# First attention in five units a batch with packed diagonal squares, up-biases with the experts' weights, rotations by one projection and a shuffle

## The chip, the cores and the metric

One core of a Trainium2 chip runs the whole program. The metric is the device time of one execution in microseconds, the median of several runs of the same kernel.

## The reference, cut to what matters

Two layers over x of 32 batches x 256 tokens x 128 channels, float32. The change is in layer 0:

```python
xn = layernorm(x)
# attention without softmax, 16 heads of 8 channels
q1, k1, q2, k2 = (rotary((xn @ W.T).reshape(B, T, 16, 8)) for W in (Wq1, Wk1, Wq2, Wk2))
v = (xn @ Wv.T).reshape(B, T, 16, 8)
# rotary on halves of a head: y1 = x1*cos + x2*sin ; y2 = -x1*sin + x2*cos
s1, s2 = q1 @ k1, q2 @ k2                      # per head, 256 x 256
pattern = where(causal, s1 / 8 * (s2 / 8), 0)
s = (pattern @ v) @ Wout.T
# gate: 8 experts, best 2 of each token, sigmoid scores
up = xn @ up_w[e] + up_b[e]                    # 128 -> 512
eo = gelu(up) @ down_w[e] + down_b[e]
g = silu(shared_expert(xn) + 0.1 * sum(w_e * eo_e))
x = x + s * g
```

Layer 1 (a strided softmax attention and a second mixture of experts) is as it was.

## The kernel before, in words

The kernel is written by hand for each engine: `tensor_program` (TensorE, PE), `vector_program` (VectorE, DVE), `scalar_program` (ScalarE, ACT), `gpsimd_program` (GpSimd, POOL) and `sync_program` (SyncE, SP, which issues most DMAs, all on one hardware queue). Each is one list of instructions in order, tied to the others by semaphores, so an engine that waits holds up all that stands behind in its own list.

**Stages.** 0 to 51 us: x is loaded, normalised, turned onto channels (XT), and values and gate logits are made (L1655 to L1663). 51 to 519 us: the first attention. To 767 us: 71 slabs of 256 rows through the experts (`expert_pe`, L1871 up and L1880 down; weights by L443, rows by L469). Then the shared expert and end of layer 0, and from 915 us on layer 1.

**The first attention** runs over 32 batches (NB) in NU = 6 x 32 units. The 256 keys x 256 queries of a batch are taken as three pairs of 128-blocks: keys low/queries low, low/high, high/high. The fourth pair lies above the diagonal and is left out. Two units make a pair, and each does 8 heads: a head group r (32 channels, four heads) stands on 32 partitions, and the queries are held in QM in four masked copies, one a head, so that one product of 32 rows x 128 keys with 4 x 128 = 512 columns gives the scores of four heads. A unit has two of these products of each kind (s1 and s2), t = 0 and 1, on row groups 2(n%2) + t, each into a PSUM bank of its own. `score_units` (L1684) issues in each step, for t = 0, 1: s1 of the next unit, then s2 of this one. The next and this unit use different row groups, so a step's four products stand on the four row groups of the array (shape 32*128 in the profile).

ScalarE copies s1 of a unit out of PSUM (L823, two instructions of 512 columns), GpSimd sets what lies above the diagonal to zero in the four units of the diagonal pairs (`causal`, L663, with a lower bound of zero), VectorE multiplies by s2 into PP (L1538), and `weigh_first` (L1708, shape 128*32) multiplies with the values VM: for each pair 16 products of 128 columns, four column groups side by side. VM is a masked copy of the values (L814), and the result is copied out once a batch (L989).

**Rotations.** Each of the four (q1, k1, q2, k2 of a batch) is two projections of 256 columns (`projection`, L1648 by W and L1649 by W with the halves of each head swapped on the host), one VectorE product of 512 columns with cos and sin (L1280), and a sum, for keys on VectorE (L1285), for queries on GpSimd (`query_sum`, L657). ScalarE makes the four masked copies of the queries (L801). They are made one to two batches ahead.

**Beside it** the gate's routing advances on VectorE by a table (`route_step`), with counts and ranks on TensorE in `ROUTED_BY` batches, and from unit 56 on GpSimd sends 2 x 64 x 128 rows to the experts' lists by 128 indirect DMAs (L630). The last steps of the routing build a table UB of the up-biases of each slab (L1214 to L1225, eight rounds), which `expert_act` reads; `s.ub` is raised after it, and `expert_weights` waits for that.

**The queue of SP** at the start: x, W0, cos/sin, then 17 DMAs of zeros into xd and 8 into yd (L578), then up_b (L580), two small matrices of the ranks (L581, L582), then a wait for all zeros, `turn_counts` (L506), weights, and rows of the experts.

## Time and profile before

| | |
|---|---|
| median of 3 runs | 1614.48 us (1612.23 to 1617.23) |
| the profiled execution's own time | 1612.6 us |
| its span, first to last instruction | 1611.4 us |
| PE / PE weight loads / DVE / ACT / POOL busy | 94% / 69% / 61% / 61% / 52% |
| first attention | 51 to 519 us |
| PE busy in it | 453.55 of 468 us |

Busy time is not work at peak: products are pipelined and a record's end is modelled, so starts of successive groups say more than lengths. A float32 product leaves two records on PE and two weight loads: the 192 x 4 products of `score_units` are 1536 records in the rows below.

### The profile page before, as it was taken

Reading aid. Unit: us, or ns where it says so; the run is one execution under the profiler, and the core shown is the slowest. Engines: PE = TensorE matmul, PEld = TensorE weight load, DVE = VectorE, ACT = ScalarE, POOL = GpSimd, SP = SyncE. Lnnn points to the kernel's source line nnn. Section 1 sums busy time; section 2 is a strip of 40 time slices with the busy share of each in tenths; the row PEclk is TensorE's granted clock in tenths of the full one; section 3 lists DMA queues with packets and bytes.
Section 4 is the critical chain, followed back from the end, with each engine's and each line's share of the span. In section 5 each row is a group of like instructions: output and inputs, shape, how many; then the busy total and the mean of one; then the engine's idle time right before and its main releaser. Section 6 shows DMA issues by size and latency. Waiting matters only on the chain.

```text
span 1611.4 us, 46794 instructions
## 1 busy us (share of the span) xinstructions
PE 1517.2 (94%) x18059; PEld 1107.6 (69%) x18059; DVE 981.5 (61%) x2063; ACT 986.3 (61%) x2039; POOL 831.8 (52%) x908
## 2 busy tenths in 40 slices
PE   7999999999999999999999889999998999999895
PEld 5545454555544999999778656666666999997663
DVE  6788898877776222222599968756664222225887
ACT  5766666777766555445455557677776545455773
POOL 7334488888875555555112210277764555553433
PEclk9999999999999999999999989999999999999998
DMA  9910002110002899999344320011113545532434
GB/s 314 418 66 2 7 30 78 51 32 30 30 26 36 217 247 253 253 247 240 92 118 118 85 56 3 15 48 47 47 43 55 95 91 99 93 76 80 133 108 126
DMA packets 296954, 169.45 MB, mean 105 GB/s; under 512 B 198080, under 2 KB 273216, under 8 KB 293792
## 3 DMA queue, kind: packets, MB, share of 16 engines
...
## 4 chain that ended last, share of the span: by engine, by line
PE 63%; POOL 12%; issue 10%; DVE 7%; ACT 4%; DMA 2%; SPq 1%; POOLq 0%; DVEq 0%; ACTq 0%
PE ps L1880 14%; PE ps L1871 14%; POOL xd L630 6%; POOL s_S L663 4%; PE ps L1684 4%; PE ps L1775 4%; PE ps L1812 4%; PE ps L1912 4%; ACT s_PX L889 3%; PE ps L1900 3%; DVE s_RS L1350 3%; PE ps L1708 2%; PE ps L1822 2%; PE ps L1841 2%; PE ps L1648 2%
## 5 line engine op out<-in xcount | busy, mean ns | idle before, releaser
L630 POOL DMA_INDIRECT xd<-s_XN,s_slots x256 | 251.7, 983 | 83.9 <-issue 62.3
L823 ACT ACTIVATE s_S<-ps 128x512 f32<-128x512 f32 x384 | 208.4, 595 | 141.3 <-PE ps L1684 141.3
L1538 DVE TENSOR_TENSOR s_PP<-ps,s_S 128x1024 f32<-128x1024 f32 x192 | 234.4, 1221 | 74.1 <-PE ps L1684 52.7
L1684 PE MATMUL ps<-s_QM,s_KK 32*128 32x512 f32 x1536 | 233.8, 639 | 2.7 <-ACT s_S L823 2.7
L889 ACT ACTIVATE s_PX<-ps,s_scl 128x1024 f32<-128x1024 f32 x128 | 135.7, 1111 | 110.5 <-PE ps L1822 110.5
L904 ACT ACTIVATE s_HH<-ps,s_LG 128x256 f32<-128x256 f32 x284 | 125.2, 474 | 122.0 <-PE ps L1871 122.0
L663 POOL TENSOR_SCALAR_AFFINE_SELECT s_S<-s_S 128x1024 f32<-128x1024 f32 x128 | 140.8, 1100 | 114.0 <-ACT s_S L823 113.4
L647 POOL DMA_INDIRECT yd<-s_Y,s_to x142 | 136.2, 959 | 122.2 <-DVE s_Y L1480 97.8
L1350 DVE TENSOR_REDUCE s_RS<-ps 128x8 f32<-128x1024 f32 x128 | 150.3, 1216 | 63.3 <-PE ps L1779 63.3
L904 ACT ACTIVATE s_XN<-ps,s_b1s 128x256 f32<-128x256 f32 x256 | 113.4, 474 | 115.1 <-PE ps L1871 111.1
L647 POOL DMA_INDIRECT yd<-s_XN,s_to x128 | 122.7, 959 | 117.5 <-DVE s_XN L1480 95.6
L1480 DVE TENSOR_TENSOR s_Y<-ps,s_W 128x256 f32<-128x256 f32 x71 | 30.1, 424 | 188.8 <-PE ps L1880 188.8
L1880 PEld LDWEIGHTS ps<-s_W,s_HH 128*128 128x128 f32 x1136 | 137.8, 192 | 3.6
L1880 PE MATMUL ps<-s_W,s_HH 128*128 128x128 f32 x1136 | 138.1, 275 | 0.0
L1871 PE MATMUL ps<-s_XG,s_W 128*128 128x256 f32 x568 | 134.8, 380 | 1.7 <-DMA s_W<-in_ew 1.0
L1708 PEld LDWEIGHTS ps<-s_PP,s_VM 128*32 128x32 f32 x3072 | 76.1, 109 | 84.8 <-DVE s_PP L1538 52.0
L1480 DVE TENSOR_TENSOR s_XN<-ps,s_b2s 128x256 f32<-128x256 f32 x64 | 27.2, 425 | 172.0 <-PE ps L1880 172.0
L1871 PE MATMUL ps<-s_XN,s_W 128*128 128x256 f32 x512 | 123.0, 384 | 4.1 <-DVE s_XN L1467 3.1
L1880 PEld LDWEIGHTS ps<-s_W,s_XN 128*128 128x128 f32 x1024 | 124.3, 192 | 3.3
L1880 PE MATMUL ps<-s_W,s_XN 128*128 128x128 f32 x1024 | 124.6, 275 | 0.0
L801 ACT ACTIVATE s_QM<-s_RQ,s_small 128x256 f32<-128x256 f32 x252 | 113.9, 507 | 0.4 <-issue 0.4
L1684 PEld LDWEIGHTS ps<-s_QM,s_KK 32*128 32x128 f32 x1536 | 74.1, 183 | 56.7 <-issue 56.1
...
## 6 DMA issues: line engine op xcount, KB each, us to landing
...
s_X<-xd SPq DMA_DIRECT2D x540, 32.0 KB
...
xd<-s_XN,s_slots POOLq DMA_INDIRECT x256
```

The costliest lines, as they stand in the source:

```text
L630: e.indirect_dma_start(out=xd, out_offset=bass.IndirectOffsetOnAxis(ap=m.slots[:, k, i:i + 1], axis=0), in_=m.XNp[:, i, 0:C + 1], in_offse ...
L647: e.indirect_dma_start(out=x.yd, out_offset=bass.IndirectOffsetOnAxis(ap=m.to[n][:, 2 * i + t:2 * i + t + 1], axis=0), in_=x.Y[i % 4][:, t ...
L663: e.affine_select(out=sel, in_=sel, pattern=[[0, 8], [1, P]], compare_op=ALU.is_ge, fill=0.0, base=0, channel_multiplier=-1).then_inc(s.ma ...
L801: i = e.mul(m.QM[b % 2][:, kind, j, :], m.RQ[q % 2][:], m.mk[j])
L823: e.mul(m.S1[u % 3][:, t * 512:(t + 1) * 512], m.PA[:, t * 512:(t + 1) * 512], 1.0 / 64.0).then_inc(s.ev1, 1)
L889: e.activation(m.PX[hp][:, 2 * half:2 * half + 2, :].rearrange("p r n -> p (r n)"), m.ps[:, (2 + 2 * half) * 512:(4 + 2 * half) * 512], AC ...
L904: e.activation(x.HH[i % 2][:, j, :], m.PS[j][:, 0:SL], func, bias=bias(i, j)).then_inc(s.eact, 1)
L1350: e.tensor_reduce(m.MM[b % 2][:, hf, 8 * rp:8 * rp + 8], m.ps[:, 1024 * rp:1024 * rp + 1024].rearrange("p (x n) -> p x n", x=8), AX.X, ALU ...
L1538: e.tensor_tensor(m.PP[u % 4][:], m.PB[u % 2], m.S1[u % 3][:], ALU.mult).then_inc(s.prod, 1)
L1684: return e.matmul(out, m.KK[k][32 * r:32 * r + 32, kind, kc * P:(kc + 1) * P], m.QM[k][32 * r:32 * r + 32, kind, :, qc * P:(qc + 1) * P], ...
L1871: e.matmul(PS[j][:, 0:SL], W[:, 0, j * P:(j + 1) * P], x.XG[i % 2][:], start=True, stop=True).then_inc(s.eup, 1)
L1880: ins = e.matmul(PS[4 + i % 2][:, c * P:(c + 1) * P], x.HH[i % 2][:, j, c * P:(c + 1) * P], W[:, 1, j * C:(j + 1) * C], start=(j == 0), st ...
```

## The change

1. **Units.** Five units a batch (UB = 5). The 64 x 64 squares on the diagonal of both diagonal pairs are packed into unit 0: all four head groups, keys 0 to 63 of each block, queries 0 to 63, with two head groups side by side in the halves of 128 partitions (`scores_packed`, products of 32 rows x 64 keys x 256 columns). Units 1 and 2 hold queries 64 to 127 of each block against all 128 keys of it (`scores_high`, two products of 256 columns in place of one of 512), units 3 and 4 the low/high pair as before (`scores_across`). The order inside `score_units` stays: t = 0: s1 of the next, s2 of this; t = 1 the same.
2. **Weighing.** `weigh_packed` (64 rows x 32 columns, 32 products of 64 columns, halved over two steps), `weigh_high` (32 products of 64 columns), `weigh_across` (16 of 128). Packed ones with c odd take the values from partitions 64 to 127, so the values of partitions 0 to 63 are moved there by four small DMAs a batch in SP's queue (`moved_values`), each waited for by `weigh_packed` through `s.v2`.
3. **Mask.** Three whole selects a batch with base 64, and a fourth on 64 partitions for the packed unit, which waits for the first.
4. **Rotations.** One projection of 256 columns; the DVE product reads it twice by a stride of zero; STREAM_SHUFFLE on VectorE exchanges the halves of each head on partitions (256 columns), then a subtraction.
5. **Biases.** up_b stands behind the experts' weights (EW 1152 to 1156 words), so the table UB and the DMA of up_b go.
6. **Schedules** of routing, counts and scatters follow the five units. In SP's queue `moved_values(0)` stands ahead of the wait for the zeros and `moved_values(1)` behind it; `turn_counts` comes at batch 4, the first five experts' weights at batch 10.

```diff
--- before.py
+++ after.py
-NU = NB * 6
+UB = 5
+NU = NB * UB
...
-ROUTED_BY = [6, 7, 8, 9]
+ROUTED_BY = [5, 6, 7, 8]
...
+def moved_values(e, m, s, b):
+
+    g = b // 2
+    e.wait_ge((s.va, s.vd)[g % 2], g // 2 + 1)
+    e.wait_ge(s.zvm, 3)
+    if b >= 1:
+        e.wait_ge(s.pv, 3 * (b - 1) + 1)
+    for h in range(4):
+        src = m.RS[0:64, b * 256:b * 256 + 256].rearrange("p (k r h d) -> p r h k d", k=4, r=2, h=4)[:, 1, h, :, :]
+        e.dma_start(m.VM[b % 2][64:128, 2, h:16:4, 8 * h:8 * h + 8], src).then_inc(s.v2, 16)
...
     e.wait_ge(s.const, 96)
-    e.dma_start(m.upb[:], a["up_b"].rearrange("e (p j) -> p e j", j=4)).then_inc(s.upb, 16)
     e.dma_start(m.r0.low[:], a["c_low"].bitcast(BF16)).then_inc(s.const, 16)
     e.dma_start(m.r0.ones[:], a["c_ones"].bitcast(BF16)).then_inc(s.const, 16)
-    e.wait_ge(s.zero, 272)
-    e.wait_ge(s.zero_y, 128)
-    turn_counts(e, m, s, m.r0, 0)
-    for i in range(m.x0.NWB):
-        expert_weights(e, m, s, i)
+    for b in range(NB):
+        moved_values(e, m, s, b)
+        if b == 0:
+            e.wait_ge(s.zero, 272)
+            e.wait_ge(s.zero_y, 128)
+        if b == ROUTED_BY[0] - 1:
+            turn_counts(e, m, s, m.r0, 0)
+        if b == 10:
+            for i in range(m.x0.NWB):
+                expert_weights(e, m, s, i)
...
     if q >= 2:
         e.wait_ge(s.qm, q - 1)
-    e.tensor_tensor(m.RQ[q % 2][:], rt[:, 0:256], rt[:, 256:512], ALU.add).then_inc(s.rq, 1)
+    e.tensor_tensor(m.RQ[q % 2][:], rt[:, 0:256], m.QX[:], ALU.subtract).then_inc(s.rq, 1)
 
 
 def causal(e, m, s, u):
-    sel = m.S1[u % 3][:].rearrange("p (b q) -> p b q", q=P)
+    sel = m.S1[u % 3][:].rearrange("p (b q) -> p b q", q=64)
     e.wait_ge(s.ev1, 2 * u + 2)
-    e.affine_select(out=sel, in_=sel, pattern=[[0, 8], [1, P]], compare_op=ALU.is_ge, fill=0.0, base=0,
+    e.affine_select(out=sel, in_=sel, pattern=[[0, 16], [1, 64]], compare_op=ALU.is_ge, fill=0.0, base=64,
                     channel_multiplier=-1).then_inc(s.mask, 1)
+    if u % UB == 0:
+        low = sel[0:64, :, :]
+        e.wait_ge(s.mask, 4 * (u // UB) + 1)
+        e.affine_select(out=low, in_=low, pattern=[[0, 16], [1, 64]], compare_op=ALU.is_ge, fill=0.0, base=0,
+                        channel_multiplier=-1).then_inc(s.mask, 1)
 
 
 def windows(e, m, s, b):
@@ -725,12 +741,12 @@
     places(e, m, s, m.x0, 0, 1)
     scatters = scatter_steps()
...
-    e.tensor_tensor(rt[:], m.PS[7], m.cs[:], ALU.mult).then_inc(s.rt, 1)
-    if x % 2 == 1:
+    e.tensor_tensor(rt[:].rearrange("p (k n) -> p k n", k=2), bcast(m.PS[7][:, 0:256], 1, 2),
+                    m.cs[:].rearrange("p (k n) -> p k n", k=2), ALU.mult).then_inc(s.rt, 1)
+    e.wait_ge(s.rt, i + 1)
+    if x % 2 == 0:
+        e.stream_shuffle(m.QX[:], rt[:, 256:512], [p ^ 4 for p in range(32)]).then_inc(s.swapped, 1)
+    else:
         if b >= 2:
-            e.wait_ge((s.sc1, s.sc2)[x // 2], (12, 6)[x // 2] * (b - 1))
-        e.wait_ge(s.rt, i + 1)
-        e.tensor_tensor(m.KK[b % 2][:, x // 2, :], rt[:, 0:256], rt[:, 256:512], ALU.add).then_inc(s.ka, 1)
+            e.wait_ge((s.sc1, s.sc2)[x // 2], (2 * UB, UB)[x // 2] * (b - 1))
+        e.stream_shuffle(m.KX[:], rt[:, 256:512], [p ^ 4 for p in range(32)]).then_inc(s.swapped, 1)
+        e.wait_ge(s.swapped, i + 1)
+        e.tensor_tensor(m.KK[b % 2][:, x // 2, :], rt[:, 0:256], m.KX[:], ALU.subtract).then_inc(s.ka, 1)
...
-    e.matmul(m.PS[7][:, 0:256], m.W0[:, 2 * x, :], xt, start=True, stop=True)
-    e.matmul(m.PS[7][:, 256:512], m.W0[:, 2 * x + 1, :], xt, start=True, stop=True).then_inc(s.proj, 1)
+    e.matmul(m.PS[7][:, 0:256], m.W0[:, x, :], xt, start=True, stop=True).then_inc(s.proj, 1)
...
+def scores_packed(e, m, k, kind, out, t):
+
+    for x in range(2):
+        for half in range(2):
+            r, at = 2 * t + half, P * x
+            i = e.matmul(out[64 * half:64 * half + 64, 256 * x:256 * x + 256], m.KK[k][32 * r:32 * r + 32, kind, at:at + 64],
+                         m.QM[k][32 * r:32 * r + 32, kind, :, at:at + 64], start=True, stop=True, skip_group_check=True)
+    return i
+
+
+def scores_high(e, m, k, kind, out, r):
+
+    for x in range(2):
+        i = e.matmul(out[:, 256 * x:256 * x + 256], m.KK[k][32 * r:32 * r + 32, kind, x * P:(x + 1) * P],
+                     m.QM[k][32 * r:32 * r + 32, kind, :, x * P + 64:(x + 1) * P], start=True, stop=True, skip_group_check=True)
+    return i
+
+
+def scores_across(e, m, k, kind, out, r):
+
+    return e.matmul(out, m.KK[k][32 * r:32 * r + 32, kind, 0:P], m.QM[k][32 * r:32 * r + 32, kind, :, P:2 * P],
+                    start=True, stop=True)
+
...
-        k, pair, r = (n // 6) % 2, (n % 6) // 2, 2 * (n % 2) + t
-        kc, qc = (0, 0, 1)[pair], (0, 1, 1)[pair]
+        k, v = (n // UB) % 2, n % UB
         out = (m.PB[n % 2] if kind else m.PA)[:, t * 512:(t + 1) * 512]
-        return e.matmul(out, m.KK[k][32 * r:32 * r + 32, kind, kc * P:(kc + 1) * P],
-                        m.QM[k][32 * r:32 * r + 32, kind, :, qc * P:(qc + 1) * P], start=True, stop=True)
+        if v == 0:
+            return scores_packed(e, m, k, kind, out, t)
+        if v < 3:
+            return scores_high(e, m, k, kind, out, 2 * (v - 1) + t)
+        return scores_across(e, m, k, kind, out, 2 * (v - 3) + t)
...
+def weigh_packed(e, m, s, b, heads):
+
+    PP = m.PP[(UB * b) % 4]
+    e.wait_ge(s.prod, UB * b + 1)
     e.wait_ge(s.vm, b + 1)
-    if pair == 0 and b >= 1:
+    e.wait_ge(s.v2, 64 * (b + 1))
+    if b >= 1:
         e.wait_ge(s.yt, b)
     for h in heads:
-        for c in range(4):
-            i = e.matmul(m.PS[6][32 * c:32 * c + 32, qc * P:(qc + 1) * P], m.VM[b % 2][:, kc, 4 * c + h, :],
-                         m.PP[(2 * q + c // 2) % 4][:, (c % 2) * 512 + h * P:(c % 2) * 512 + (h + 1) * P],
-                         start=(pair == 0 and h == 0), stop=(h == 3 and pair != 1), skip_group_check=True)
+        for x in range(2):
+            for c in range(4):
+                at = 512 * (c // 2) + 256 * x + 64 * h
+                lanes = slice(64 * (c % 2), 64 * (c % 2) + 64)
+                values = m.VM[b % 2][lanes, 2, 8 * x + 4 * (c // 2) + h, :] if c % 2 else m.VM[b % 2][lanes, x, 4 * c + h, :]
+                i = e.matmul(m.PS[6][32 * c:32 * c + 32, P * x:P * x + 64], values, PP[lanes, at:at + 64],
+                             start=(h == 0 and x == 0), stop=(h == 3 and x == 0), skip_group_check=True)
     if heads[-1] == 3:
         i.then_inc(s.pv, 1)
+
+
+def weigh_high(e, m, s, b):
+
+    e.wait_ge(s.prod, UB * b + 3)
+    for h in range(4):
+        for x in range(2):
+            for c in range(4):
+                at = (c % 2) * 512 + 256 * x + 64 * h
+                i = e.matmul(m.PS[6][32 * c:32 * c + 32, P * x + 64:P * x + 128], m.VM[b % 2][:, x, 4 * c + h, :],
+                             m.PP[(UB * b + 1 + c // 2) % 4][:, at:at + 64], start=False, stop=(h == 3 and x == 0),
+                             skip_group_check=True)
+    i.then_inc(s.pv, 1)
+
+
...
-        q, heads = pair_of(u)
-        if v == 5 and b + 2 < NB:
-            projection(e, m, s, b + 2, 1)
-        if q is not None:
-            weigh_first(e, m, s, q, heads)
         if v == 0 and b + 1 < NB:
             projection(e, m, s, b + 1, 2)
-        if v == 2 and b + 1 < NB:
-            projection(e, m, s, b + 1, 3)
-        if v == 3 and b + 2 in ROUTED_BY:
-            e.wait_ge(s.rt, 4 * (b + 1) + 4)
-            stage = ROUTED_BY.index(b + 2)
+        if v == 1 and b >= 1:
+            weigh_across(e, m, s, b - 1)
+        if v == 1 and b + 1 in ROUTED_BY:
+            e.wait_ge(s.rt, 4 * (b + 1) + 3)
+            stage = ROUTED_BY.index(b + 1)
             if stage == 0:
                 route_counts(e, m, s, m.r0, 0)
             elif stage == 1:
                 route_total(e, m, s, m.r0)
             else:
                 route_ranks(e, m, s, m.r0, 0, stage - 2)
+        if v == 2 and b + 1 < NB:
+            projection(e, m, s, b + 1, 3)
+        if v in (2, 3) and b < NB:
+            weigh_packed(e, m, s, b, (2 * v - 4, 2 * v - 3))
+        if v == 3 and b + 2 < NB:
+            projection(e, m, s, b + 2, 0)
+        if v == 4:
+            weigh_high(e, m, s, b)
         if v == 4 and b + 2 < NB:
-            projection(e, m, s, b + 2, 0)
+            projection(e, m, s, b + 2, 1)
```

## Rows read from the trace of the kernel before

**Rows 1.** Windows: the first attention and a part of the experts, busy us of each engine.

```profile
51.00:519.00 468.00, 453.55 (x5103) 233.29 (x5105) 384.14 (x453) 323.12 (x701) 312.39 (x318) 1.00 0.18 60
560.00:640.00 80.00, 80.00 (x547) 75.25 (x547) 18.15 (x49) 40.27 (x92) 43.13 (x46) 1.00 0.97 250
```

**Rows 2.** Timeline of PE, one batch: start us, us, instructions merged by line.

```profile
299.60 1.34 PE L1684 MATMUL ps<-s_QM,s_KK 32*128 32x512 f32 x8
300.87 0.70 PE L1648 MATMUL ps<-s_XT,s_W 128*128 128x256 f32 x2
...
301.93 1.14 PE L1684 MATMUL ps<-s_QM,s_KK 32*128 32x512 f32 x8
...
305.71 0.64 PE L1708 MATMUL ps<-s_PP,s_VM 128*32 128x128 f32 x16
306.28 0.70 PE L1648 MATMUL ps<-s_XT,s_W 128*128 128x256 f32 x2
...
307.34 1.14 PE L1684 MATMUL ps<-s_QM,s_KK 32*128 32x512 f32 x8
...
312.82 1.08 PE L1708 MATMUL ps<-s_PP,s_VM 128*32 128x128 f32 x32
313.84 1.34 PE L1684 MATMUL ps<-s_QM,s_KK 32*128 32x512 f32 x8
```

**Rows 3.** Costliest groups of 51 to 517 us: busy us, mean ns, idle before.

```profile
L1538 DVE TENSOR_TENSOR s_PP<-ps,s_S 128x1024 f32<-128x1024 f32 x191 | 233.2, 1221 | 73.1 <-PE ps L1684 52.7 <-PE ps L1708 13.4 <-POOL s_S L663 5.0
L663 POOL TENSOR_SCALAR_AFFINE_SELECT s_S<-s_S 128x1024 f32<-128x1024 f32 x128 | 140.8, 1100 | 114.0 <-ACT s_S L823 113.4
L630 POOL DMA_INDIRECT xd<-s_XN,s_slots x128 | 127.7, 998 | 30.6 <-issue 28.8 <-DVE s_slots L1159 1.4 <-POOL s_XN L636 0.3
L1648 PE MATMUL ps<-s_XT,s_W 128*128 128x256 f32 x244 | 84.9, 429 | 10.0 <-DVE s_RT L1280 9.4 <-DVE s_r0TS L1142 0.3
L657 POOL TENSOR_TENSOR s_RQ<-s_RT 128x256 f32<-128x256 f32 x61 | 45.1, 739 | 9.0 <-DVE s_RT L1280 7.8
```

**Rows 4.** Timeline of PE in the experts, where no shape changes.

```profile
564.23 1.89 PE L1871 MATMUL ps<-s_XG,s_W 128*128 128x256 f32 x8
565.96 0.27 PE L1880 MATMUL ps<-s_W,s_HH 128*128 128x128 f32 x1
```

**Rows 5.** Timeline of PE, the batch of rows 2, cut so that one score group falls apart into its records.

```profile
302.46 0.61 PE L1684 MATMUL ps<-s_QM,s_KK 32*128 32x512 f32 x4
303.00 0.70 PE L1648 MATMUL ps<-s_XT,s_W 128*128 128x256 f32 x2
```

**Rows 6.** Timeline of PE in layer 1: weighing products of 64 columns.

```profile
1108.55 1.10 PE L1841 MATMUL ps<-s_PX,s_VN 128*32 128x64 f32 x64
1109.58 0.39 PE L1812 MATMUL ps<-s_Q,s_KS 32*128 32x128 f32 x4
```

**Rows 7.** Line L1467: the nearest VectorE instruction to a shuffle; min/median/max ns.

```profile
L1467 DVE STREAM_TRANSPOSE s_XG<-s_X x71: 403/435/447, 518.2 to 763.1; 128x256 f32<-128x256 f32 x71
```

**Rows 8.** Timeline of SP's queue at the start: start us, us to issue.

```profile
64.62 2.21 SPq L580 DMA_DIRECT2D s_upb<-in_up_b  x1
66.88 18.21 SPq L581 DMA_DIRECT2D s_r0low<-in_c_low  x1
85.14 1.02 SPq L582 DMA_DIRECT2D s_r0ones<-in_c_ones  x1
```

**Rows 9.** DMA issues: KB each, median us from issue to landing.

```profile
s_r0low<-in_c_low SPq DMA_DIRECT2D x1, 32.0 KB, 20.7
s_r0ones<-in_c_ones SPq DMA_DIRECT2D x1, 32.0 KB, 5.1
```

**Rows 10.** Timeline of SP's queue: issues of rows' DMAs in the experts.

```profile
601.60 2.01 SPq L469 DMA_DIRECT2D s_X<-xd  x4
```

**Rows 11.** Timeline of PE: the first weighing of batch 0.

```profile
61.22 1.08 PE L1708 MATMUL ps<-s_PP,s_VM 128*32 128x128 f32 x32
```

**Rows 12.** Windows around a sparse stretch of PE: its granted clock is the last but two.

```profile
930.00:935.00 5.00, 3.24 (x23) 2.78 (x29) 2.82 (x12) 2.37 (x6) 0.00 (x0) 0.50 0.00 0
```

More of the change, by code:

```diff
@@ L53, in route_step @@
 def route_step(u):
-    if u < 25:
-        return 2 if u % 6 in (1, 3) else 0
-    if u < 61:
-        return {25: 1, 27: 1, 31: 1, 33: 1, 37: 1, 39: 1, 43: 1, 45: 1, 49: 2, 51: 1, 55: 1}.get(u, 0)
-    return 1 if u % 6 in (1, 3) else 0
+    if u < 20:
+        return {0: 1, 1: 2, 3: 1}.get(u % UB, 0)
+    return {20: 1, 21: 1, 23: 1, 26: 2, 31: 1, 33: 1, 36: 2, 38: 1, 40: 1, 41: 1, 43: 1, 45: 1}.get(u, 0)
 def scatter_steps():
     steps, n = {}, 0
-    for u in range(56, NU):
-        for _ in range((1, 1, 2, 1, 1, 0)[u % 6]):
-            if n < 2 * NT and (n != NT or u % 6 == 0):
+    for u in range(42, NU):
+        for _ in range((1, 1, 2, 2, 0)[u % UB]):
+            if n < 2 * NT and (n != NT or u % UB == 2):
                 steps.setdefault(u, []).append((n % NT, n // NT))
@@ L262, in memory @@
     m.PP = [sbx(at, f"PP{k}", [P, 1024]) for k in range(4)]
-    m.VM = [sbx(at, f"VM{k}", [P, 2, 16, 32]) for k in range(2)]
+    m.VM = [sbx(at, f"VM{k}", [P, 3, 16, 32]) for k in range(2)]
+    m.KX = sbx(at, "KX", [P, 256])
+    m.QX = sbx(at, "QX", [P, 256])
     at.close()
@@ L389, in semaphores @@
     s.v_seq = sem("v_seq")
-    s.const, s.upb, s.sw, s.zero, s.w0, s.c1, s.bb = (sem("l_" + n) for n in ("const", "upb", "sw", "zero", "w0", "c1", "bb"))
+    s.const, s.v2, s.sw, s.zero, s.w0, s.c1, s.bb = (sem("l_" + n) for n in ("const", "v2", "sw", "zero", "w0", "c1", "bb"))
     s.zero_y, s.placed, s.to, s.nb, s.norm_a, s.norm_p, s.cnt_row = (sem(n) for n in (
@@ L1203, in gate_first @@
     o.mark(e.tensor_tensor(m.big[:], bcast(m.tix, 1, E), bcast(base[:, 1, :], 2, 72), ALU.is_ge))
-    eid, oh = (sc[:].rearrange("p i e -> p (i e)")[:, 72 * q:72 * (q + 1)] for q in range(2))
+    eid = sc[:].rearrange("p i e -> p (i e)")[:, 0:72]
     o.wait()
@@ L1210, in gate_first @@
     o.wait()
[L1211 removed]
+    e.tensor_copy(m.idxb, eid).then_inc(s.ub, 1)
     yield
[L1213 to L1226 removed]
 def gate_second(e, m, s, o):
@@ L1541, in vector_program @@
                 rotate(e, m, s, b + 1, 2 + v // 2)
-            if v in (4, 5) and b + 2 < NB:
-                rotate(e, m, s, b + 2, v - 4)
+            if v in (3, 4) and b + 2 < NB:
+                rotate(e, m, s, b + 2, v - 3)
         for _ in range(route_step(u)):
             next(gate, None)
-    expert_dve(e, m, s, o, m.x0, 0, lambda i: m.x0.all[i % 5][:, 2 * HID:EW])
+    expert_dve(e, m, s, o, m.x0, 0, lambda i: m.x0.all[i % 5][:, 2 * HID:2 * HID + C])
     e.wait_ge(s.sw, 80)
@@ L1938, in end_pe, with products_of_zeros @@
         i.then_inc(s.lg1, 1)
-def products_of_zeros(e, m, n):
+def products_of_zeros(e, m, n, bank=6):
     for _ in range(n):
-        e.matmul(m.PS[6], m.zero[:, 0:P], m.zero[:, 0:512], start=True, stop=True)
+        e.matmul(m.PS[bank], m.zero[:, 0:P], m.zero[:, 0:512], start=True, stop=True)
 def tensor_program(e, m, s):
@@ L1968, in tensor_program @@
             values_logits(e, m, s, 2 * k + q)
-    for u in range(-1, NU + 4):
-        v, b = u % 6, u // 6
+    for u in range(-1, NU + 2):
+        v, b = u % UB, u // UB
         if u < NU:
@@ L2172 @@
     g = {k: np.asarray(v) for k, v in inputs.items()}
-    swap = np.array([(c // 8) * 8 + (c % 8 + 4) % 8 for c in range(P)])
     mats = []
```

104 lines of the change are left out of this document (44 added, 60 removed).

## The prediction

> **What bounds it now.** I read the windows first: in the first attention PE is busy 453.55 of 468 us, against 384 for DVE, 323 for ACT and 312 for POOL [rows 1]. Busy records on PE overlap, so I then read its timeline by starts [rows 2]. From 299.60 to 313.84 us one batch (six units) goes by, and each group starts where the one before leaves off; no row there has idle time before it. That sum is 14.24 us; 32 of them are 456 of the 468 us, and the other 12 are waits, 9.4 of them of a projection for the DVE product that reads its bank [rows 3]. POOL stands idle 113.4 us until ACT has copied scores [rows 3], and ACT has 145 us of its own to spare [rows 1]. So a stage of the change is worth what it does to PE's list, until another engine's own sum per batch passes it. The experts behind it are full on PE too (80.00 of 80 us, DMA share 0.97 [rows 1]); the change leaves their instructions alone but for 4 words in 1152 of a weights' row, 0.35% of one DMA, which I set at 0, with 3 us as bound if DMA became the limit there.
>
> **The price of a group on PE.** In the experts, where no shape changes, 8 records of 256 columns take 565.96 - 564.23 = 1.73 us [rows 4]: 0.216 a record, 0.43 a float32 product of 256 columns. Two projections take 301.93 - 300.87 = 1.06 us [rows 2], which is 2 x 0.43 + 0.20. A score group (four products of 512 columns on four row groups) takes 303.00 - 301.93 = 1.07 us [rows 2, 5], which is the 0.86 of one product, since all four run side by side, + 0.21. Sixteen weighing records take 306.28 - 305.71 = 0.57, thirty-two 313.84 - 312.82 = 1.02 [rows 2], so 0.44 by sixteen + 0.13. In layer 1, 64 records of 64 columns take 1109.58 - 1108.55 = 1.03 [rows 6]: halving the columns halves the price. So **each change of shape costs about 0.2 us, in which nothing streams**. Between 128*32 and 128*128, where only the columns differ, it is there too: two projections behind a weighing take 307.34 - 306.28 = 1.06, as they do behind scores.
>
> **Part by part, one batch on PE.**
> - *Projections*: four products instead of eight. One costs 0.43 + 0.21 = 0.64; four 2.56 instead of 4.24.
> - *Weighing*: across 1.02, high (64 records of 64 columns) 1.03, packed two halves of 32 such records, 0.57 each: 3.2, as before (2 x 1.02 + 2 x 0.57).
> - *Scores, steps 1 to 3* (of v = 0 to 4): one shape, 32*128. Step 3 has four row groups at once as before: 1.07. Steps 1 and 2 have two products of 256 columns behind one another in a row group, but different row groups can run beside them: the cut timeline shows that the first records of all four products of a group start ahead of the second record of any of them (four of the eight start at 302.46, 0.53 us behind the first four at 301.93 [rows 2, 5]), so a record that waits for its row group lets others by. I take 1.07 for each.
> - *Scores, steps 0 and 4*: here the t-loop alternates whole shapes: s1 of 32*128 and s2 of 32*64 in step 0, the reverse in step 4. No row shows these two shapes next to each other. Bounds: below, no cost of a change, then the busiest row group streams four products of 256 columns, 4 x 0.43 + 0.21 = 1.93. Above, each of the four phases stands alone, two products long: 4 x (0.86 + 0.21) = 4.28. I take the upper, because every neighbouring pair of shapes in rows 2 has the 0.2 us, those that differ in columns alone too.
> - Sum: 3 x 1.07 + 2 x 4.28 + 2.56 + 3.2 = **17.5 us** against 14.24: +3.25 a batch, **+104 us**. The unit that was saved on ACT, DVE and POOL is paid on PE, since a packed group has no partner of its own shape.
>
> Other engines in a batch: DVE was busy 384 / 32 = 12.0 us [rows 1]; one product of 1.22 [rows 3] goes and four shuffles come. The shuffle is in no row; nearest is STREAM_TRANSPOSE on the same 128 x 256 words, 0.43 [rows 7]; bounds 0.40, its lowest, and 1.22, the product of four times the words. Sum 12.0 - 1.2 + 1.7 = 12.5, hidden under 17.5, and 15.7 by the upper bound still is. ACT, 323 / 32 = 10.1, loses a sixth of its score copies: hidden. POOL 4 selects of 1.10 [rows 3] (a select on 64 partitions taken like one on 128), 2 sums of 0.74, 6 scatters of 0.98 = 11.8, hidden. Should the PE cover be only 12.8 (rival below), POOL with 0.2 us ahead of each scatter (28.8 us of issue by 128 [rows 3]) needs 13.0. The eight bias rounds go from DVE, some 12 us off the path; 0. The DMA of up_b leaves SP (2.21 us [rows 8]); 0, since what follows is blocked by the zeros anyway. The waits of projections for DVE halve: -5.
>
> **SP's queue.** `weigh_packed` of batch 0 waits for four DMAs that stand behind all 25 zero DMAs. In rows 8 the fills are issued until 64.6 us, the next small DMA then holds SP for 18.21 us, and r0ones goes out at 85.14 and lands 5.1 us later [rows 9], at 90. The first small one took 20.7 us to land [rows 9], so nothing overtakes the zeros on that queue. Four moves of about 0.5 us issue each (four row loads: 2.01 us [rows 10]) follow r0ones: landed at about 91. PE gets to the packed weighing of batch 0, which stood at 61.22 [rows 11], at about 62.5. It stops there, and with it every list: **+29 us**. Bounds: 0 if the moves overtook the zeros, 32 if they land with 5 us each behind 88. Later moves have from step 3 of one batch to step 2 of the next, over 9 us even at 12.8 a batch, for 2 us of issue and some 2 of flight: 0. Those of batch 5 stand behind `turn_counts` and its DVE wait, those of 11 behind five weights' DMAs at the same place; both have most of a batch: 0. After a stretch in which PE worked little, its granted clock stood at 0.50, the 1.2 GHz level [rows 12]; a restart after 29 us idle I price at +3.
>
> Sum against the profiled execution's 1612.6 us: 104 + 29 + 3 - 5 = +131, **1743.6 us**; the median shown, 1614.5, stands 1.9 above that execution, so I give 1745. Its own range is 1713 (no stop) to 1765.
>
> **Rivals.**
> 1. *The two widths of column share the array without a gap.* Then steps 0 and 4 are 1.93, a batch 12.8 on PE and 13.1 with POOL's list; 32 x 13.1 + 7 of waits + 32 for the stop = 458 against 468: 1603, and 1572 without the stop. For it: the 32*64 and 32*128 products leave free row groups to each other, which no pair in rows 2 does. Against: the gap in rows 2 does not ask what changes. Chance 0.26.
> 2. *Order within one shape.* If a product that waits for its row group holds up those behind it, step 1 is five and step 2 three products of 0.43 in a row (2.36 and 1.50), +1.7 a batch, and a batch takes 19.2: 1800, on top of my own case. Without the shape gaps it would be 17.1 a batch, 1731. Against it stands the start of 302.46 in rows 5. The Trainium skill (TensorE: Matmul & The Clock Gate, Part 3, what overlaps) says that matmuls start and end in strict program order; by that rule this case is the one to expect, and the trace disagrees for the two records of one product. Chances 0.13 with the gaps, 0.04 without.
> 3. *Packed row groups write one bank and take turns.* In `scores_packed` and `weigh_packed` neighbours differ in row group but share a bank, which no row of before shows. Taking turns would double the packed score phases (4 x 0.86 = 3.4 more) and make the packed weighing four times as long (2.6 more): +6 a batch, 1938. The Trainium skill (TensorEngine Tiling (Array Packing), Gotcha 1) states that different row tiles cannot access the same PSUM bank at the same time; no row here can show it. Chance 0.04.
>
> The side is decided at the steps with two shapes: at (14.6 x 32 - 32 - 7) / 32 = 13.4 us a batch the change breaks even, which is a step of 2.25 us, near the lower bound.
>
> **How the numbers follow.** My case 0.50, rivals 0.26, 0.17 and 0.04, unexplained 0.03. Only rival 1 is faster (0.24, with 0.04 for a result within 0.3%, about what a measurement of this kernel can tell from no change); slower 0.72. The range leaves out rival 3, the worse half of rival 2 and rival 1 without a stop: 1590 to 1785.
>
> **What would show it.** In the timeline of PE the step with s1 of 32*64 should last 4.3 us with gaps of 0.2 between its four phases, the batch 17.5; 1.9 would be rival 1. Score steps 1 and 2 of 1.07 show that order does not bind, 2.4 and 1.5 that it does. PE should stop from about 62 to 91 us with the DMA of s_VM as releaser; SP's timeline should show those issues behind 85 us. Were that wait short, 29 us of the sum would be wrong. DVE's shuffles at 0.43 test only their own price.

## The result and the profile after

The changed kernel takes 1840.69 us (median of 4 runs, 1839.51 to 1849.51) against 1613.36 us for the kernel before on the same chip (1610.27 to 1617.23): **1.142 times as long, 95% interval 1.138 to 1.146**. The forecast was 1745 us and its range ended at 1785. In a later set of runs the same two kernels gave 1839.66 and 1611.03 us, 1.141 [1.136, 1.145].

In the two sets of runs that hold e5 to e13 the kernel before itself took 1673 us instead of 1612, with PE waiting for its own instructions; every ratio below is against the kernel before of the same set.

The windows of the changed kernel, the first attention whole, then its part behind the stop, then a stretch of the experts (us, busy us of PE, PE weight loads, DVE, ACT, POOL with instructions, PE clock, DMA share, GB/s; [rows 1] before):

```profile
51.00:748.60 697.60, 669.72 (x7944) 368.04 (x7944) 379.08 (x642) 299.01 (x639) 319.62 (x320) 0.80 0.14 42
88.70:748.60 659.90, 658.93 (x7857) 361.25 (x7859) 368.33 (x622) 288.74 (x615) 312.58 (x313) 0.81 0.10 22
```

The first expert product starts at 748.6 us in place of 519.3, which is 229 us later; the whole kernel is 229 us longer in its span (1840.1 against 1611.4). So all of it lies in the first attention. PE is busy throughout, as before, but its granted clock is 0.80 where [rows 1] has 1.00. The slices of the changed kernel's profile page show that it lasts through this stage and ends with it:

```profile
PEclk9778878788888877999999999899999999999998
```

Each digit is 46 us: the second to the sixteenth are the first attention; behind them one slice of layer 1 and the last one have an 8, the others a 9.

One batch in a stretch at full clock (timeline of PE: start us, us, records merged by line; L1677 is `scores_packed`, L1685 `scores_high`, L1692 `scores_across`, L1744, L1757 and L1769 the three weighings, L1655 the projection; [rows 2] before):

```profile
307.39 1.08 PE L1677 MATMUL ps<-s_QM,s_KK 32*64 32x256 f32 x8
308.39 1.12 PE L1692 MATMUL ps<-s_QM,s_KK 32*128 32x512 f32 x2
309.44 1.08 PE L1677 MATMUL ps<-s_QM,s_KK 32*64 32x256 f32 x8
310.45 1.12 PE L1692 MATMUL ps<-s_QM,s_KK 32*128 32x512 f32 x2
311.51 1.10 PE L1757 MATMUL ps<-s_PP,s_VM 128*32 128x64 f32 x64
312.54 0.70 PE L1655 MATMUL ps<-s_XT,s_W 128*128 128x256 f32 x2
313.17 1.12 PE L1685 MATMUL ps<-s_QM,s_KK 32*128 32x256 f32 x4
...
317.30 0.70 PE L1655 MATMUL ps<-s_XT,s_W 128*128 128x256 f32 x2
317.92 1.17 PE L1685 MATMUL ps<-s_QM,s_KK 32*128 32x256 f32 x16
319.02 1.08 PE L1769 MATMUL ps<-s_PP,s_VM 128*32 128x128 f32 x32
...
321.92 0.65 PE L1744 MATMUL ps<-s_PP,s_VM 64*32 64x64 f32 x32
322.50 1.20 PE L1692 MATMUL ps<-s_QM,s_KK 32*128 32x512 f32 x8
...
324.83 1.08 PE L1677 MATMUL ps<-s_QM,s_KK 32*64 32x256 f32 x8
```

From 307.39 to 324.83 us a batch takes 17.44 us. Steps 4 (307.39 to 311.51) and 0 (313.17 to 317.30) take 4.12 and 4.13, in four phases of 1.0 to 1.06 each. One batch later the same groups (step 0) look like this:

```profile
331.80 2.07 PE L1685 MATMUL ps<-s_QM,s_KK 32*128 32x256 f32 x4
333.80 1.97 PE L1677 MATMUL ps<-s_QM,s_KK 32*64 32x256 f32 x8
335.70 2.07 PE L1685 MATMUL ps<-s_QM,s_KK 32*128 32x256 f32 x4
```

Each phase is 1.9 to 2.0 us from start to start: the granted clock from 330 to 340 us is 0.50, the level of 1.2 GHz. The instructions and their order are the same, and no row has idle time ahead of it.

At the first packed weighing PE stops, and SP's queue has its DMAs of the moved values (L437) behind those of the zeros (two fences, timelines of PE and of SP; compare [rows 8, 11]):

```profile
62.59 0.70 PE L1655 MATMUL ps<-s_XT,s_W 128*128 128x256 f32 x2
88.70 1.08 PE L1744 MATMUL ps<-s_PP,s_VM 64*32 64x64 f32 x32 [25.41 <-DMA s_VM<-s_RS]
```

```profile
64.47 2.18 SPq L587 DMA_DIRECT2D s_r0low<-in_c_low  x1
66.69 2.17 SPq L588 DMA_DIRECT2D s_r0ones<-in_c_ones  x1
68.97 52.15 SPq L437 DMA_DIRECT2D s_VM<-s_RS  x12
```

**The sum.** 32 batches of 17.44 us are 558.1. The stage from 51 us lasts 697.6, of which 1.6 lie ahead of its first products and 25.4 are the stop. 697.6 - 1.6 - 25.4 - 558.1 = 112.5 us are left, and that I put down to the low clock. The other way: a mean clock of 0.81 over the 659.9 us behind the stop, with levels of 1.0 and 0.5, means 0.38 of that time at the lower one, half of which is lost: 125 us. The two agree to 13 us.

No other engine is near. VectorE waits 275.6 us ahead of its products for PE, ScalarE 393.0 ahead of its score copies (costliest groups of the stage; [rows 3] before):

```profile
L1545 DVE TENSOR_TENSOR s_PP<-ps,s_S 128x1024 f32<-128x1024 f32 x159 | 194.2, 1221 | 275.6 <-PE ps L1677 122.6 <-PE ps L1692 95.4 <-PE ps L1685 54.7
L839 ACT ACTIVATE s_S<-ps 128x512 f32<-128x512 f32 x320 | 180.8, 597 | 393.0 <-PE ps L1685 283.5 <-PE ps L1677 58.8 <-PE ps L1692 50.7
```

### The profile page after: what moved, and what is told of

Same layout as the page of the kernel before. It is cut to its first block, busy times and chain, and to the rows that moved or that the text cites. A ratio compares the mean times of both kernels' runs of the same rounds, so it can differ in the third digit from the quotient of the medians.

```text
span 1840.1 us, 52522 instructions
## 1 busy us (share of the span) xinstructions
PE 1733.5 (94%) x20871; PEld 1242.0 (67%) x20875; DVE 979.9 (53%) x2262; ACT 960.7 (52%) x1975; POOL 837.3 (46%) x908
## 4 chain that ended last, share of the span: by engine, by line
PE 80%; DVE 6%; SPq 5%; ACT 3%; issue 2%; DMA 2%; POOL 0%; DVEq 0%; POOLq 0%; ACTq 0%
PE ps L1939 12%; PE ps L1930 12%; PE ps L1685 9%; PE ps L1677 8%; PE ps L1692 7%; PE ps L1655 5%; PE ps L1834 3%; PE ps L1871 3%; PE ps L1971 3%; DVE s_RS L1357 3%; PE ps L1959 3%; ACT s_PX L905 3%; PE ps L1769 2%; SPq L585 2%; PE ps L1757 2%
## 5 line engine op out<-in xcount | busy, mean ns | idle before, releaser
L839 ACT ACTIVATE s_S<-ps 128x512 f32<-128x512 f32 x320 | 180.8, 597 | 393.0 <-PE ps L1685 283.5
L1545 DVE TENSOR_TENSOR s_PP<-ps,s_S 128x1024 f32<-128x1024 f32 x160 | 195.4, 1221 | 276.0 <-PE ps L1677 122.6
L641 POOL DMA_INDIRECT xd<-s_XN,s_slots x256 | 248.0, 969 | 91.2 <-issue 70.2
L674 POOL TENSOR_SCALAR_AFFINE_SELECT s_S<-s_S 128x1024 f32<-128x1024 f32 x96 | 110.5, 1151 | 210.0 <-ACT s_S L839 209.8
L1685 PE MATMUL ps<-s_QM,s_KK 32*128 32x256 f32 x1024 | 196.6, 546 | 0.8 <-ACT s_S L839 0.8
L920 ACT ACTIVATE s_HH<-ps,s_W 128x256 f32<-128x256 f32 x284 | 125.1, 473 | 122.4 <-PE ps L1930 122.4
L1685 PEld LDWEIGHTS ps<-s_QM,s_KK 32*128 32x128 f32 x1024 | 119.8, 261 | 61.9 <-issue 41.7
L1677 PE MATMUL ps<-s_QM,s_KK 32*64 32x256 f32 x1024 | 160.3, 438 | 0.2 <-DVE s_KK L1292 0.2
L1692 PE MATMUL ps<-s_QM,s_KK 32*128 32x512 f32 x512 | 153.8, 668 | 0.9 <-ACT s_S L839 0.9
L1677 PEld LDWEIGHTS ps<-s_QM,s_KK 32*64 32x64 f32 x1024 | 66.2, 145 | 85.4 <-issue 45.1
```

Of the source, the lines that this page charges most:

```text
L641: e.indirect_dma_start(out=xd, out_offset=bass.IndirectOffsetOnAxis(ap=m.slots[:, k, i:i + 1], axis=0), in_=m.XNp[:, i, 0:C + 1], in_offse ...
L839: e.mul(m.S1[u % 3][:, t * 512:(t + 1) * 512], m.PA[:, t * 512:(t + 1) * 512], 1.0 / 64.0).then_inc(s.ev1, 1)
L920: e.activation(x.HH[i % 2][:, j, :], m.PS[j][:, 0:SL], func, bias=bias(i, j)).then_inc(s.eact, 1)
L1545: e.tensor_tensor(m.PP[u % 4][:], m.PB[u % 2], m.S1[u % 3][:], ALU.mult).then_inc(s.prod, 1)
L1677: i = e.matmul(out[64 * half:64 * half + 64, 256 * x:256 * x + 256], m.KK[k][32 * r:32 * r + 32, kind, at:at + 64], m.QM[k][32 * r:32 * r ...
L1685: i = e.matmul(out[:, 256 * x:256 * x + 256], m.KK[k][32 * r:32 * r + 32, kind, x * P:(x + 1) * P], m.QM[k][32 * r:32 * r + 32, kind, :, x ...
```

## The experiments

Theory 1: in steps 0 and 4 only one or two of the array's four row groups are in use at a time (a call of `scores_packed` uses two, one of `scores_high` or `scores_across` one), for 8.25 of 17.44 us, and this both lengthens the steps and takes the clock. Rivals: a batch holds fewer products on the whole array, four projections in place of eight, and that takes the clock (2); the stop at 62 to 88 us starts a low clock that then stays (3). In the texts on e5 and e6 theory 1 is called 1a, and 1b is a further rival: the many changes of shape take the clock.

**e1, products kind by kind.** In the steps with two shapes both halves of s1 go out ahead of both of s2. The packed products then stand on all four row groups. The others of these steps (one unit, t = 0 and 1) stand on two in place of one, so e1 does not fill the array everywhere: some 1.05 us of such a step still uses two row groups.

```diff
-    for t in range(2):
+    turns = [(0, 0), (1, 0), (0, 1), (1, 1)]
+    if u % UB in (0, UB - 1):
+        turns = [(0, 0), (0, 1), (1, 0), (1, 1)]
+    for kind, t in turns:
```

> The changed kernel with one edit: in the two steps of a batch in which the score products have two shapes, all products of one shape are issued before those of the other. Theory 1 (the alternation costs 2 us a step, and the low use of the array in its phases takes the clock down): these steps go from 4.12 to about 2.1 us, a batch from 17.44 to 13.4 us at full clock, and the granted clock in the first attention comes back to about 1.00, so 51 + 25 (the stop, still there) + 32 x 13.4 + 8 = 513 us to the end of the stage against 749, and a time of about 1605. Theory 2 (the clock falls since the batch holds fewer products on the whole array): the steps shorten as well but the clock stays near 0.83, the stage then takes some 20% more of 429 us, about 1690. Theory 3 (the stop at 63 us throws the clock into a pattern that it keeps): as theory 2, about 1690.

Measured: 1628.15 us against 1611.91, 1.008 [1.005, 1.011]. This one reordering takes 212 us off the changed kernel. The clock is back, though the stop is still there and even longer (29.5 us). Right behind it, from 88 to 92 us, both kernels stand at 0.50; from 104 to 112 us the changed kernel is at 0.50 and e1 at 1.00. So theory 3, by which the stop alone sets the low clock going, falls here. Theory 2 falls as well, as e1 has the same four projections a batch (windows as above):

```profile
120.00:200.00 80.00, 73.20 (x1301) 42.87 (x1301) 73.52 (x129) 47.60 (x105) 31.36 (x30) 0.96 0.04 5
200.00:300.00 100.00, 96.72 (x1806) 57.94 (x1802) 85.22 (x145) 64.40 (x142) 81.67 (x82) 1.00 0.22 61
```

To 200 us, while routing runs on VectorE beside the rotations, DVE (73.5 of 80 us) is as full as PE. I hadn't priced that. It is part of the 23 us by which e1 came out above its expectation: up to 200 us projections wait 7.1 us in all, each time for VectorE. The other holes of PE and the 0.96 are not split up.

**e2, the moved values early.** Those of batches 0 to 2 are issued from ScalarE's queue, ahead of SP's wait for the zeros.

```diff
+        if v == 4 and b < 2:
+            moved_values(e, m, s, b + 1)
```

> The changed kernel with one edit: the moved values of batches 0 to 2 are sent from ScalarE's queue, not behind the zeros in SP's. All theories: the wait of PE for the DMA of s_VM, 25.4 us at 63 us, goes to under 3. Theory 1 and 2: the clock in the rest of the stage stays near 0.83, time about 1840 - 25 - 3 = 1812. Theory 3 (the stop starts the pattern of the clock): the clock stays at 1.00, about 1840 - 25 - 110 = 1705.

Measured: 1818.27 us, 1.127 [1.124, 1.131]; clock 0.79, 0.84 and 0.81 in the windows 90:120, 120:200 and 200:300. (The profiled run took 1837.97 us, more than the median.) The stop went from 25.4 to 14.1 us, where under 3 had been expected, so e2 by itself doesn't test theory 3. It shows that a shorter stop leaves the low clock as it was.

**e3, both.**

> The changed kernel with both edits (products ordered by shape, first moves on ScalarE's queue). Theory 1: the clock at 1.00 and no stop, a batch of 13.4 us, 1605 - 27 = about 1578, faster than both kernels. Theory 2: about 1660.

Measured: 1622.72 us, 1.006 [1.004, 1.009], and once more, as e17, 1622.64 against 1611.03, 1.007 [1.005, 1.010]; the expectation of e3, 1578, was missed by 45 us. The clock is 1.00 from 90 to 400 us, but the stop was only cut in two, not taken away (timelines of PE and of ScalarE with its DMA issues):

```profile
60.94 2.48 PE L1687 MATMUL ps<-s_QM,s_KK 32*128 32x256 f32 x16 [4.03 <-ACT s_S L838]
...
81.32 1.08 PE L1749 MATMUL ps<-s_PP,s_VM 64*32 64x64 f32 x32 [14.00 <-DMA s_VM<-s_RS]
```

```profile
55.06 0.69 ACTq L437 DMA_DIRECT2D s_VM<-s_RS  x1
55.46 0.39 ACT L829 COPY s_VM<-s_RS 128x256 f32<-128x256 f32 x1
55.78 4.37 ACTq L437 DMA_DIRECT2D s_VM<-s_RS  x3
60.20 1.08 ACT L838 ACTIVATE s_S<-ps 128x512 f32<-128x512 f32 x2 [4.35 <-issue]
```

The four small DMAs, issued from 55.06 to 60.15 us on another engine's queue, were of use only at 81.3: they too wait behind the zeros (e7 below takes the zeros out of their way, and the wait goes). And issuing the last three held ScalarE for 4.4 us.

> Both edits of the first call. 1620 to 1625 us with a kernel before at about 1613 us, 1830 to 1860 us with one at about 1673 us, if the difference of the two calls lies in the chip's state alone.

**e4, the rotation alone**, put into the kernel before: one projection, the product that reads it twice, the shuffle.

```diff
-    e.matmul(m.PS[7][:, 256:512], m.W0[:, 2 * x + 1, :], xt, start=True, stop=True).then_inc(s.proj, 1)
+        e.stream_shuffle(m.QX[:], rt[:, 256:512], [p ^ 4 for p in range(32)]).then_inc(s.swapped, 1)
```

> The kernel before with one part of the change alone: one projection for a rotation and the shuffle on VectorE. PE's batch goes from 14.24 to 14.24 - 4 x 0.43 = 12.5 us, VectorE's sum (6 x 1.22 + 4 x 0.68 + 4 x 0.43 + 2 x 0.43 to 0.68) to about 13, so a batch of about 13.3 instead of 14.6 and a time of about 1613 - 40 = 1573, with the clock at 1.00 by theory 1. By theory 2 (fewer products on the whole array take the clock down) the clock in the stage falls below 0.95 and the time comes to 1600 or more.

Measured: 1625.12 us, 1.008 [1.005, 1.011], 52 us above the expectation by theory 1. A late batch takes 13.28 us on PE in place of 14.24, as expected. But the shuffles make VectorE the limit:

```profile
120.00:200.00 80.00, 69.70 (x791) 32.18 (x793) 76.13 (x133) 51.10 (x111) 30.91 (x32) 0.96 0.01 2
200.00:300.00 100.00, 84.92 (x916) 39.02 (x912) 90.12 (x151) 60.92 (x132) 69.38 (x70) 0.91 0.10 31
```

DVE is busy 76.13 of 80 and 90.12 of 100 us there, PE has holes, and its clock is a little lower (0.96 and 0.91) in the same windows. From 300 to 500 us, with PE busy for over 96% of the time and half the projections, it is 0.98 and 0.99, above the 0.95 of theory 2. So the rotation alone doesn't pay. The five units take a product of 1.22 us a batch off VectorE, which should leave room for it, but no run has the five units without the rotation.

**e5 and e6, fewer row groups in the kernel before.** All score products from row groups 0 and 1, or from 0 alone; the heads of the other groups are left out. The order and the number of changes of shape are those of the kernel before.

```diff
-        k, pair, r = (n // 6) % 2, (n % 6) // 2, 2 * (n % 2) + t
+        k, pair, r = (n // 6) % 2, (n % 6) // 2, t
```

(`0` in place of `t` for e6.) A product for the same row group waits for the one before it, so the steps also get longer (1.92 us in e5 at full clock, 1.07 in the kernel before).

> The kernel before, but every unit takes its scores from head groups 0 and 1 (heads of groups 2 and 3 are left out, those of 0 and 1 are taken twice), so that the four products of a step share two row groups; the shapes and their changes are those of the kernel before. A step goes from 1.07 to 0.21 + 2 x 0.86 = 1.93 us, a batch from 14.24 to 19.4 at full clock, so the stage ends at 51 + 32 x 19.4 + 12 = 684 us. Theory 1a (less of the array in use takes the clock down): the granted clock in the stage falls below 0.95 and the stage ends at 700 to 800. Theory 1b (it is the many changes of shape, not the use of the array): the clock stays at 1.00, the end at 684. If a product that waits for its row group holds up those behind it, a step is 2.8 us and the end at about 850 even at full clock.

> As the run with two row groups, with all scores from head group 0, so the four products of a step stand behind one another in one row group: a step 0.21 + 4 x 0.86 = 3.65 us, a batch 29.7, end of the stage at 1014 us at full clock. Theory 1a: the clock falls further than with two row groups, the end at 1100 or later. Theory 1b: clock 1.00, end at 1014.

Measured (one run each, against 1674.38): 1973.81 and 2926.22 us. The first expert product starts at 824.9 and at 1775.3 us, later than any end expected at full clock (684 and 1014). Windows and the clock's slices of e5 (49 us a digit), then a window of e6:

```profile
51.00:200.00 149.00, 148.23 (x930) 69.19 (x930) 81.31 (x100) 68.68 (x141) 36.38 (x38) 0.77 0.25 102
200.00:400.00 200.00, 191.95 (x1572) 94.12 (x1571) 122.09 (x165) 107.16 (x218) 96.27 (x97) 0.98 0.09 29
400.00:600.00 200.00, 192.75 (x1174) 89.51 (x1173) 78.39 (x88) 78.45 (x158) 85.24 (x89) 0.73 0.05 15
PEclk9579999958868887699999999999999989999998
```

```profile
200.00:400.00 200.00, 200.00 (x599) 85.36 (x598) 49.12 (x60) 40.65 (x81) 21.10 (x22) 0.53 0.00 1
```

With one row group PE's records fill 200.00 of 200 us and the clock is 0.53; with four it is 1.00 [rows 1]. Shapes change as often in all three, and less often per microsecond in the slower ones, so e6 speaks for few row groups (1a) and against changes of shape (1b). e1 alone doesn't separate them, as it halves the number of phases of these steps too. With two row groups it goes both ways: e5 stands at 1.00 from 140 to 380 us and at 0.50 from 60 to 120 and from 400 to 440, with the same steps throughout. What tips it there is not shown. That fits e1, which keeps two row groups for a sixth of its batch and stays near 1.00.

e5 also tests the order: its 1.92 us (303.11 to 305.03) are the 1.93 expected if a product that waits lets others by; otherwise it would be 2.8.

**e7 and e9, zeros spread out.** e1's order, and on SP's queue 3 of the 25 DMAs of zeros, the moves of batches 0 and 1, six more, then three behind the moves of each next batch. e9 also puts the routing steps further apart and 5 units later.

```diff
+    fill(3)
+    moved_values(e, m, s, 0)
+    moved_values(e, m, s, 1)
+    fill(6)
...
+    for b in range(2, NB):
         moved_values(e, m, s, b)
+        if b < 9:
+            fill(3)
```

> The changed kernel with the products ordered by shape, the moved values of batches 0 and 1 sent behind three of the 25 zero DMAs, and the rest of the zeros sent behind the moved values of batches 1 to 8 in threes. The stop at 60 to 90 us should be gone (under 3 us of waits for the DMA of s_VM in all), the stage end at 51 + 32 x 13.66 + 12 (waits for VectorE while the routing runs) = 500 us against 519 before and 522 with the first moves on ScalarE's queue: a time of about 1597. Rival: the moves are held up by the DMAs of zeros ahead of them in each batch, and the stop only moves: 1615 or more.

> The same with the routing's steps on VectorE thinned out (3 instead of 4 a batch at first) and all that follows from them five units later. If VectorE's list bounds the batches up to 200 us (95% busy there with the first moves on ScalarE's queue), the stage ends some 8 us earlier, about 1590; if not, the same time as without it.

Measured: 1820.26 us, 1.086 [1.077, 1.094], and 1809.3, 1.078 [1.071, 1.085], more than 200 us above both expectations. Up to 200 us it goes as expected: PE is busy 28.09 of the 30 us from 60 to 90 in e7, at clock 1.00 and a DMA share of 0.29, and the stop is gone. Behind 200 us PE waits for its own instructions in the packed weighings (timeline of PE, e7):

```profile
302.70 0.52 PE L1761 MATMUL ps<-s_PP,s_VM 64*32 64x64 f32 x10
303.65 0.33 PE L1761 MATMUL ps<-s_PP,s_VM 64*32 64x64 f32 x4 [0.43 <-issue]
...
306.59 0.46 PE L1761 MATMUL ps<-s_PP,s_VM 64*32 64x64 f32 x4 [1.13 <-issue]
...
```

The 32 records of such a half take 0.58 us elsewhere and 5.7 here (302.70 to 308.42), and the clock is 0.83 from 200 to 300 us. Was it the spreading, or that set of runs?

**e10, e11 and e12: the same three kernels (e7, e9, e3) once more, and e13, the biases alone** put into the kernel before.

```diff
-EW = 2 * HID + C
+EW = 2 * HID + C + 4
```

> The kernel of e7_fills_spread once more, beside the kernel with the first moves on ScalarE's queue, since in its first call the kernel before took 1674 us, 62 more than in the call ahead of it, and PE had 159 us of waits for its own instructions in the packed weighing that the other kernels did not show. If that was a state of the chip, the kernel before is back near 1612 and this one takes about 1597; if these waits belong to the kernel, it stays near 1820 beside a kernel before of 1612.

> The kernel of e9_fills_spread_routing_later once more, for the same reason: about 1590 if the waits for instructions were a state of the chip and VectorE's list bounds the first nine batches, the same as e10_spread_again if it does not.

> The kernel of e3_both once more, as the thing to compare with in this call: 1.006 times the kernel before, as it was. If the chip is in the state of the second call, it too takes some 1.08 times the kernel before.

> The kernel before with one part of the change alone: the up-biases behind the experts' weights, without the table on VectorE and without the DMA of up_b. All theories: no difference that can be measured (within 0.3%), since VectorE's 12 us stand beside a full PE and the weights' rows grow by 0.35% only.

Measured, against 1672.56: e10 1834.48 (1.096 [1.091, 1.101]), e11 1829.7 (1804.59 to 1843.94), e12 1843.17 (1.100 [1.093, 1.108]), e13 1671.35 (0.999 [0.997, 1.000]). e12 is e3, which had 1.006 before, and e10 to e12 show the same waits as e7: so the loss goes with those sets of runs and not with the spreading. These sets ran on two different chips, one of them the chip of e1 to e4 and of e14 to e17, so the loss is not that of one chip either. The biases with the weights cost nothing and give nothing, though DVE's busy time in 51:519 goes from 384.14 [rows 1] to 365.59 us. In e13 the first attention is intact (first expert product at 523.4 us against 519.3). The lost 60 us lie in layer 1, in its weighing of 64 columns: ahead of it the engine is idle for 87 us in e13 and for 25 in the kernel before. Its weight loads between 1000 and 1500 us, e13, then the kernel before:

```profile
L1825 PEld LDWEIGHTS ps<-s_PX,s_VN 128*32 128x32 f32 x2368 | 40.2, 110 | 41.4 <-issue 39.0 <-ACT s_PX L887 1.9
```

```profile
L1841 PEld LDWEIGHTS ps<-s_PX,s_VN 128*32 128x32 f32 x2624 | 38.8, 110 | 8.1 <-issue 4.0 <-ACT s_PX L889 1.6
```

Both places have short records, 64 columns each. But that can't be all: the high weighing has records of 64 columns too and waited only 3.0 us for instructions in e12, where the packed one waited 60.

**e14 to e16: the changed kernel, e7 and e9 once more**, in a set where the kernel before was back at 1611.03.

> The changed kernel as it is, again. If the waits of TensorE for its own instructions belong to the state of the chip and meet every packed kernel (A), a kernel before at about 1673 us goes with a changed kernel at 1900 us or more; if they come only with the order kind by kind, whose groups of like records are longer (B), the changed kernel stays at about 1.14 times the kernel before minus the 60 us that the latter has lost elsewhere, at 1900 us with its first attention still ending at 745 to 755 us. With the kernel before at about 1613 us neither is tested, and 1835 to 1850 us is expected.

> Kind by kind, and the fills of zeros spread between the moves. With a kernel before at about 1613 us and no waits for instructions: 20 us under the version with both edits of the first call (1623), so 1595 to 1610 us, a little faster than the kernel before. A rival: VectorE sets the first 200 us in any case, and the late batches give 0.6 us each only, so 1613 to 1625 us. With a kernel before at about 1673 us: 1820 to 1835 us as twice before, and nothing new.

> The same with routing spread thinner and later. With a kernel before at about 1613 us: 1585 to 1605 us if routing on VectorE holds the first 200 us, the same as the spread version within 5 us if it doesn't. With a kernel before at about 1673 us: 1805 to 1830 us as twice before.

Measured: e14 1839.66 (1.141 [1.136, 1.145]; it doesn't test A against B); **e15 1600.9, 0.993 [0.991, 0.996]; e16 1594.0, 0.990 [0.987, 0.993]**. Both beat the kernel before, by less than 1% but clear of the interval. A batch of e15 (timeline of PE; step 4 from 308.47 to 310.57, step 0 from 312.27 to 314.37):

```profile
303.67 0.69 PE L1706 MATMUL ps<-s_QM,s_KK 32*128 32x512 f32 x1
...
308.47 1.11 PE L1691 MATMUL ps<-s_QM,s_KK 32*64 32x256 f32 x16
309.51 1.13 PE L1706 MATMUL ps<-s_QM,s_KK 32*128 32x512 f32 x4
310.57 1.14 PE L1774 MATMUL ps<-s_PP,s_VM 128*32 128x64 f32 x64
311.64 0.70 PE L1669 MATMUL ps<-s_XT,s_W 128*128 128x256 f32 x2
312.27 1.14 PE L1699 MATMUL ps<-s_QM,s_KK 32*128 32x256 f32 x8
313.33 1.11 PE L1691 MATMUL ps<-s_QM,s_KK 32*64 32x256 f32 x16
314.37 0.70 PE L1669 MATMUL ps<-s_XT,s_W 128*128 128x256 f32 x2
...
317.11 0.69 PE L1706 MATMUL ps<-s_QM,s_KK 32*128 32x512 f32 x1
```

The two steps take 2.10 us each in place of 4.13, the batch 13.44 in place of 17.44, and 14.24 before. 0.8 x 32 = 26 us, of which e16 keeps 21 at the start of the experts (497.9 us against 519.3) and 17 in the end. The e15 and e16 windows of 90:120 and of 120:200 show what holds the rest, and where e16 gains on e15:

```profile
90.00:120.00 30.00, 26.19 (x466) 15.45 (x462) 29.18 (x50) 18.66 (x42) 12.57 (x12) 0.98 0.58 222
120.00:200.00 80.00, 74.39 (x1337) 43.39 (x1339) 73.08 (x127) 47.65 (x105) 39.54 (x38) 0.96 0.29 102
```

```profile
90.00:120.00 30.00, 28.97 (x540) 17.02 (x536) 29.03 (x50) 19.38 (x43) 12.56 (x12) 1.00 0.60 225
120.00:200.00 80.00, 72.09 (x1340) 42.76 (x1334) 76.35 (x131) 47.45 (x104) 40.52 (x39) 1.00 0.28 98
```

VectorE is full (29 of 30, 76.35 of 80 us) until routing is through.

## Why the prediction was right in direction and wrong in size

- **The step that failed** is the term "a restart after 29 us idle I price at +3" and with it the unspoken one that every other term was taken from rows at full clock. In its place stand 112 us of low clock, spread over the whole stage. 1743.6 + 109 is 1853, 12 above the measured time; the other terms make that up (waits 6, stop 4, batch 2). [Rows 12] had been read as a thing of sparse stretches of PE. But the records of the packed steps leave no hole (658.93 of 659.90 us busy), and the clock is low all the same. e1 shows that the order of the products in steps 0 and 4 makes the difference, and e6 that PE's records can fill the time at 0.53 when one row group works. That it is the number of row groups and not another side of that order is the reading that fits e1, e5 and e6; e5 shows that two row groups do not take the clock at all times. The prediction had worked out the very steps in which it happens and asked of them only how long they last.
- **PE's batch**: 17.5 predicted, 17.44 measured. Steps 0 and 4: 4.28 each, measured 4.13 and 4.12. Projections 0.64, measured 0.63; the packed weighing 0.57, measured 0.58 (321.92 to 322.50); step 1 1.07, measured 1.10; step 2, as the cut timeline has it, 1.26 (320.03 to 321.29).
- **The stop**: 29 predicted, 25.4 measured, at the place and with the releaser named. SP was not held for 18 us by one small DMA this time; it issued the moves from 68.97 us and they lay in the queue instead, which comes to nearly the same end, 88.7 in place of 91.
- **Waits of projections for DVE**, -5: the way is right and the size too small. The stage before had 12 us beyond its 32 batches, the stage after has 1.6 beside the stop and the clock, so some 11 went, and PE's projections have 0.0 us of idle ahead of them. In e15 with a batch of 13.4 waits are there again (7.7 us for the product on VectorE).
- **Shuffle** 0.43 predicted from the transpose; 0.434 and 0.436 measured as means. Hidden under 17.44 as said; e4 shows what it costs once that cover is gone.
- **Biases** 0: e13, 0.999.
- **Rival 1** (widths share the array without a gap) fell: each phase starts 1.0 us behind the last. **Rival 2** (order within one shape) fell: step 1 has sixteen records of two products to a row group and takes 1.10 us, not 2.36, and e5 says the same. The rule of the Trainium skill (TensorE: Matmul & The Clock Gate, Part 3) that matmuls start and end in strict program order would give 2.36; the trace disagrees. **Rival 3** fell: 0.58 us for 32 packed weighing records, 1.0 for a packed score phase. The Trainium skill's rule on one PSUM bank (TensorEngine Tiling (Array Packing), Gotcha 1) doesn't show here, where the row groups write different partitions of the bank.
- The break-even of the prediction, a step of 2.25 us with the stop in place (2.22 by its own figures), was a little too high: e1 has 2.10 and the stop, and came out at 1.008. The prediction's sum has no waits for VectorE in the first 200 us; e1 has them.
- **Luck**: the side of the forecast, slower, came from the gaps between the shapes, and they are there: 102 us of the 229. The clock, which no term held, was worth more than that.

**Still open**: what starves PE of instructions in some sets of runs, and whether the changed kernel as it is would suffer from it. What tips the clock with two row groups in use (e5) is open, and the later routing of e16 was not tried in the kernel before.
